# Residual rows kept in two load buffers, and the x and z normalizations on GpSimd

## The reference

```
x1  = x  + layernorm(recurrent(layernorm(x)))
out = x1 + layernorm(ffn(layernorm(x1)))

recurrent(v): u = v @ W_in.T + b_in                  # 512 -> 1024
              s[t] = tanh(u[t] + s[t-1] * gamma + beta)   # 1024 steps, elementwise
              y = s @ W_out.T + b_out                # 1024 -> 512
ffn(v):       z = ((silu(v @ gate_w * gate_scale)) * (v @ up_w * up_scale)) @ down_w * down_scale
                                                     # 512 -> 1536 -> 512
```

## Time and profile before

| | |
|---|---|
| Median of 3 runs | 625.39 us (625.18 to 625.69) |
| The profiled execution's own time | 625.78 us |
| Its span, first to last instruction | 624.0 us |
| Busy: PE, PEld | 528.8 us (85%), 449.0 us (72%) |
| Busy: DVE | 481.0 us (77%) |
| Busy: ACT | 310.6 us (50%) |
| Busy: POOL | 240.4 us (39%) |
| Mean granted TensorE clock | 0.937 |

### The profile page before, as it was taken

How to read it: one execution, slowest core, us unless ns; L and a number is a source line. 1 busy time by engine, 2 the same in 40 slices (tenths; PEclk the granted TensorE clock), 3 DMA queues, 4 the chain that set the end, 5 groups by cost and what they waited for, 6 DMA issues and landing times.

```text
span 624.0 us, 9844 instructions
## 1 busy us (share of the span) xinstructions
PE 528.8 (85%) x2880; PEld 449.0 (72%) x2880; DVE 481.0 (77%) x1832; ACT 310.6 (50%) x1442; POOL 240.4 (39%) x320
## 2 busy tenths in 40 slices
PE   4655232878999999999999999999999992999993
PEld 4644211568977998789878987799779971798992
DVE  4999997999778667966787679767886678675734
ACT  1354423365554755576546654665466544452330
POOL 2776672555224222422333332422342224243532
PEclk9957757789999999999999999999999996999997
DMA  7453440301010200110012001100001000100000
GB/s 235 128 171 123 124 141 29 90 29 52 1 35 1 69 1 1 35 67 2 1 34 69 1 2 34 56 14 0 2 3 65 2 0 2 67 2 2 1 35 34
DMA packets 16598, 27.47 MB, mean 44 GB/s; under 512 B 2336, under 2 KB 4512, under 8 KB 16544
## 3 DMA queue, kind: packets, MB, share of 16 engines
q1 hardware_dynamic: 16544, 26.84, 13.7%
HBM read 22.63 MB, written 4.19 MB: 43 GB/s over the span
## 4 chain that ended last, share of the span: by engine, by line
DVE 57%; ACT 21%; PE 14%; issue 3%; DMA 1%; SPq 1%; POOL 1%; POOLq 0%; DVEq 0%; ACTq 0%
DVE recur L634 23%; ACT pairs L922 10%; PE gate_up L528 7%; ACT pairs L909 4%; DVE fused L728 4%; ACT sigm L942 4%; DVE gated L721 3%; PE wide L553 3%; DVE peaks L780 3%; ACT fused_hi L957 3%; PE wide L493 2%; DVE rounder_own L776 2%; DVE y L675 2%; DVE z L793 2%; DVE x_in L658 2%
## 5 line engine op out<-in xcount | busy, mean ns | idle before, releaser
L922 ACT ACTIVATE pairs<-recur 128x16 f32<-128x16 f32 x1024 | 191.2, 187 | 249.5 <-DVE recur L634 247.1
L634 DVE TENSOR_TENSOR_SCAN recur<-recur,pairs 128x32 f32<-128x32 f32 x1024 | 234.4, 229 | 101.5 <-ACT pairs L922 100.1
L1025 POOL TENSOR_TENSOR fused_lo<-fused,fused_hi 128x256 fp32r<-128x256 f32 x96 | 71.1, 741 | 180.5 <-ACT fused_hi L957 180.4
L468 PE MATMUL wide<-x_norm_t,w_in_sb 128*128 128x256 f32 x448 | 106.6, 396 | 17.5 <-ACT pairs L909 13.2
L482 PE MATMUL wide<-w_out_sb,pairs 128*128 128x512 f32 x224 | 101.3, 606 | 22.1 <-DMA w_out_sb<-w_out_t 22.1
L468 PEld LDWEIGHTS wide<-x_norm_t,w_in_sb 128*128 128x128 f32 x448 | 87.6, 199 | 34.6 <-ACT pairs L909 15.4
L482 PEld LDWEIGHTS wide<-w_out_sb,pairs 128*128 128x128 f32 x224 | 65.5, 297 | 51.8 <-DMA w_out_sb<-w_out_t 22.5
L528 PE MATMUL gate_up<-x_hi,gate_q 128*128 128x256 f32 x384 | 96.8, 285 | 1.0 <-DVE fused L728 0.6
L528 PE MATMUL gate_up<-x_lo,up_q 128*128 128x256 f32 x384 | 96.0, 283 | 0.0
L528 PE MATMUL gate_up<-x_hi,up_q 128*128 128x256 f32 x384 | 95.6, 282 | 0.0
L528 PE MATMUL gate_up<-x_lo,gate_q 128*128 128x256 f32 x384 | 94.9, 281 | 0.0
(11 more groups left out here) (75 smaller groups left out, 640.2 us busy)
## 6 DMA issues: line engine op xcount, KB each, us to landing
x_in<-x SPq DMA_DIRECT2D x16, 256.0 KB, 3.1
x_res<-x SPq DMA_DIRECT2D x16, 256.0 KB, 3.1
out<-z SPq DMA_DIRECT2D x14, 256.0 KB, 2.4
raw_own<-gate_w SPq DMA_DIRECT2D x10, 256.0 KB, 2.8
raw_own<-down_w SPq DMA_DIRECT2D x9, 256.0 KB, 2.7
w_in_sb<-w_in_t SPq DMA_DIRECT2D x4, 512.0 KB, 6.8
raw_own<-up_w SPq DMA_DIRECT2D x8, 256.0 KB, 2.7
w_out_sb<-w_out_t SPq DMA_DIRECT2D x8, 256.0 KB, 2.9
```

The source lines that it names most:

```text
L468: ins = eng.matmul(wide[bank][:, jj * TOK:(jj + 1) * TOK], w_in_sb[:, k, j * P:(j + 1) * P], x_norm_t[:, k, :], start=(k == 0), stop=(k == ...
L634: eng.tensor_tensor_scan(preact[:, part(h), :].rearrange("p c k -> p (c k)"), factors[:, part(h), :].rearrange("p c k -> p (c k)"), pairs[ ...
L922: eng.activation(pairs[:, (n * T + t) % RING, part(h), 0], preact[:, part(h), 1], ACT.Tanh).then_inc(s_state[h], 1)
L1025: eng.tensor_tensor(fused_lo[:, f, :], fused[:, f, :], fused_hi[:, f, :].bitcast(F32), ALU.subtract).then_inc(s_fused_lo, 1)
```

## The change

There are two changes.

*Buffers.* x_res becomes two buffers, used by turns, and x1 stays in the one that its rows were loaded into until the tail has added it to z. The buffer x1 and the copy `keep_x1` go. The load into x_res of block n now waits for the tail of block n - 2.

*Engines.* The normalization of x of blocks 1 to 7 and that of z of blocks 0 to 6 go from VectorE to GpSimd, at the places that they had. On GpSimd each is one small instruction that negates the mean (128x1), and one that adds it and multiplies by the root, on the whole tile (128x512), where VectorE had two halves (128x256). The first block's x and the last block's z stay as they were. Semaphore counts follow (`x_normed`, `z_normed`).

```diff
-        x_res = sb("x_res", [P, batch, dim])
+        x_res = [sb(f"x_res{i}", [P, batch, dim]) for i in range(2)]
         y = sb("y", [P, batch, dim])
-        x1 = sb("x1", [P, batch, dim])
...
+        def x_normed(tile):
+            return 2 * (tile + 1) if tile < batch else batch + tile + 1
+
+        def z_normed(tile):
+            return tile + 1 if tile < batch * LAST else 2 * (tile + 1) - batch * LAST
...
             def load_residual(n, place):
                 yield place
-                if n > 0:
-                    eng.wait_ge(s_x1_kept, n)
-                    eng.wait_ge(s_x1_norm, 2 * batch * n)
+                if n >= 2:
+                    eng.wait_ge(s_out_ready, batch * (n - 1))
                 for b in range(batch):
-                    eng.dma_start(x_res[b:P:batch, :, :], x_blocks[n][b]).then_inc(s_x_res_in, 16)
+                    eng.dma_start(x_res[n % 2][b:P:batch, :, :], x_blocks[n][b]).then_inc(s_x_res_in, 16)
...
                     strands += [scale_z(n, b, at["z_copy"][b]),
                                 measure("z", z, n, b, at["z_halves"][b], at["z_whole"][b],
-                                        (s_z_scaled, 2 * (n * batch + b + 1))),
-                                normalize_z(n, b, at["z_norm"][b])]
+                                        (s_z_scaled, 2 * (n * batch + b + 1)))]
+                    if n == LAST:
+                        strands.append(normalize_z(n, b, at["z_norm"][b]))
...
                     strands += [measure_x(n + 1, b, BEFORE) for b in range(batch)]
-                    strands += [normalize_x(n + 1, b, BEFORE["x_norm"][b]) for b in range(batch)]
...
+            def normalize(w, rows, n, b, place, done):
+                yield place
+                tile = n * batch + b
+                eng.wait_ge(s_mv[w], tile + 1)
+                eng.tensor_scalar(minus_mean[w][:, b:b + 1], mean_var[w][:, b, 0:1], -1.0, 0.0, ALU.mult,
+                                  ALU.add).then_inc(s_minus_mean[w], 1)
+                eng.wait_ge(s_minus_mean[w], tile + 1 if w == "z" else tile - batch + 1)
+                eng.wait_ge(s_rstd[w], tile + 1)
+                eng.tensor_scalar(rows[:, b, :], rows[:, b, :], minus_mean[w][:, b:b + 1], rstd[w][:, b:b + 1],
+                                  ALU.add, ALU.mult).then_inc(done, 1)
+
...
-            def keep_x1(n, place):
-                yield place
-                eng.wait_ge(s_x1, batch * (n + 1))
-                if n > 0:
-                    eng.wait_ge(s_out_ready, batch * n)
-                eng.tensor_scalar(x1[:, :, :].rearrange("p b d -> p (b d)"),
-                                  x_res[:, :, :].rearrange("p b d -> p (b d)"), 0.0, 1.0, ALU.add,
-                                  ALU.mult).then_inc(s_x1_kept, 1)
...
                     strands.append(root("z", n, b, at["z_whole"][b]))
+                    if n < LAST:
+                        strands.append(normalize("z", z, n, b, at["z_norm"][b], s_z_norm))
                     if n < LAST or b < batch - 1:
                         strands.append(add_x1(n, b, at["z_norm"][b] + 1))
...
                     strands += [root("x", n + 1, b, BEFORE["x_whole"][b]) for b in range(batch)]
+                    strands += [normalize("x", x_in, n + 1, b, BEFORE["x_norm"][b], s_x_norm) for b in range(batch)]
...
-                    strands.append(keep_x1(n - 1, at["keep"]))
```

More of the change, by code:

```diff
@@ L48 @@
 AFTER = {"y": (0, 28), "y_copy": (23, 44), "y_norm": (30, 51), "r": (36, 56), "r_norm": (41, 61),
-         "t2": (57, 65), "t2_high": (57, 66), "keep": 68}
+         "t2": (57, 65), "t2_high": (57, 66)}
 FFN = 73
@@ L57 @@
 LAST_AFTER = {"y": (0, 28), "y_copy": (23, 44), "y_norm": (30, 51), "r": (36, 56), "r_norm": (41, 61),
-              "t2": (57, 64), "t2_high": (57, 65), "keep": 68}
+              "t2": (57, 64), "t2_high": (57, 65)}
 LAST_FFN = 85
 GROUP_AFTER = {"y": (66, 0), "x_res": 72, "y_copy": (87, 15), "y_norm": (97, 19.9), "r": (104, 23),
-               "r_norm": (110, 27), "t2": (32, 32), "t2_high": (32, 34), "keep": 60}
+               "r_norm": (110, 27), "t2": (32, 32), "t2_high": (32, 34)}
 END_USE = ((0, 0.3, 0.4, 1), (2, 2.3, 2.4, 3))
@@ L189, in recurrent_sandwich_kernel @@
         var_eps = {w: sb(f"var_eps_{w}", [P, batch]) for w in "xyrz"}
+        minus_mean = {w: sb(f"minus_mean_{w}", [P, batch]) for w in "xz"}
         rstd = {w: sb(f"rstd_{w}", [P, batch]) for w in "xyrz"}
@@ L227, in recurrent_sandwich_kernel @@
         s_var_eps = {w: sem(f"s_var_eps_{w}") for w in "xyrz"}
+        s_minus_mean = {w: sem(f"s_minus_mean_{w}") for w in "xz"}
         s_rstd = {w: sem(f"s_rstd_{w}") for w in "xyrz"}
@@ L426, in transpose_x @@
                     eng.wait_ge(s_ident_in, 16)
-                eng.wait_ge(s_x_norm, 2 * (tile + 1))
+                eng.wait_ge(s_x_norm, x_normed(tile))
                 if n >= 3:
@@ L685, in normalize_x1 @@
                             eng.wait_ge(s_t2, tile - batch + 1)
-                    eng.tensor_scalar(x1_norm[:, b, halves(half)], x_res[:, b, halves(half)],
+                    eng.tensor_scalar(x1_norm[:, b, halves(half)], x_res[n % 2][:, b, halves(half)],
                                       mean_var["r"][:, b, 0:1], rstd["r"][:, b:b + 1],
@@ L709, in residual_norm @@
                         normalize_y(n, b, at["y_norm"][b]),
-                        measure("r", x_res, n, b, (at["r"][b], at["r"][b] + 1), at["r"][b] + 2, (s_x1, tile + 1)),
+                        measure("r", x_res[n % 2], n, b, (at["r"][b], at["r"][b] + 1), at["r"][b] + 2, (s_x1, tile + 1)),
                         normalize_x1(n, b, at["r_norm"][b])]
@@ L764, in add_last_residual @@
                     if half == 0:
-                        eng.wait_ge(s_z_norm, 2 * batch * NB)
-                    eng.tensor_tensor(z[:, batch - 1, halves(half)], z[:, batch - 1, halves(half)], x1[:, batch - 1, halves(half)],
-                                      ALU.add).then_inc(s_last_ready, 1)
+                        eng.wait_ge(s_z_norm, z_normed(batch * NB - 1))
+                    eng.tensor_tensor(z[:, batch - 1, halves(half)], z[:, batch - 1, halves(half)],
+                                      x_res[LAST % 2][:, batch - 1, halves(half)], ALU.add).then_inc(s_last_ready, 1)
             def convert(first, end):
@@ L1008, in add_residual @@
                     eng.wait_ge(s_x_res_in, 16 * batch * (n + 1))
-                eng.tensor_tensor(x_res[:, b, :], y[:, b, :], x_res[:, b, :], ALU.add).then_inc(s_x1, 1)
-            def keep_x1(n, place):
-                yield place
-                eng.wait_ge(s_x1, batch * (n + 1))
-                if n > 0:
-                    eng.wait_ge(s_out_ready, batch * n)
-                eng.tensor_scalar(x1[:, :, :].rearrange("p b d -> p (b d)"),
-                                  x_res[:, :, :].rearrange("p b d -> p (b d)"), 0.0, 1.0, ALU.add,
-                                  ALU.mult).then_inc(s_x1_kept, 1)
+                eng.tensor_tensor(x_res[n % 2][:, b, :], y[:, b, :], x_res[n % 2][:, b, :], ALU.add).then_inc(s_x1, 1)
             def low_parts(n, use):
@@ L1034, in add_x1 @@
                 tile = n * batch + b
-                eng.wait_ge(s_z_norm, 2 * (tile + 1))
-                eng.tensor_tensor(z[:, b, :], z[:, b, :], x1[:, b, :], ALU.add).then_inc(s_out_ready, 1)
+                eng.wait_ge(s_z_norm, z_normed(tile))
+                eng.tensor_tensor(z[:, b, :], z[:, b, :], x_res[n % 2][:, b, :], ALU.add).then_inc(s_out_ready, 1)
             def tail(n, at):
@@ L1083, in _ @@
             weave(low_parts(LAST - 1, {**end_use, **use_places(END_FFN, LAST_CHUNKS, KI, beside=False)}),
-                  *tail(LAST - 1, END_TAIL), *residual_norm(LAST, 1, GROUP_AFTER), keep_x1(LAST, GROUP_AFTER["keep"]),
+                  *tail(LAST - 1, END_TAIL), *residual_norm(LAST, 1, GROUP_AFTER),
                   low_parts(LAST, use_places(GROUP_FFN, 0, KI, beside=False)))
```

1 line of the change is left out of this document (removed).

## The result

| | before | after |
|---|---|---|
| median of the runs taken side by side | 625.43 us (625.07 to 626.18, 20 runs) | 626.46 us (625.17 to 627.26, 20 runs) |
| span of the profiled execution | 624.0 us | 624.9 us |
| VectorE instructions, busy | 1832, 481 us | 1776, 461 us |

The ratio is 1.0016 with a 95% interval of 1.0009 to 1.0022: the changed kernel is 0.16% slower, 1.0 us. The forecast was 0.5 us faster. The time lies in the forecast's wide range (621.9 to 627.6), outside its narrower one (624.0 to 626.1), and the sign is the other way, though still within the 0.2% that the forecast called no change. All ratios here are of runs in the fast state, so that two runs of the kernel before, of 1888 us, taken beside e1 to e4, are left out.

What follows compares the result with a forecast made beforehand. The recurrence, scan and tanh in turn, was taken to set the pace, with TensorE the other limit; 0.6 (blocks 2 to 7) less 0.2 (block 0) plus 0.1 (block 1), 0.5 off 625.39, gave 624.9 us, range 621.9 to 627.6.

Steps and rivals of the forecast that it cites:

- The long step at place 53: Blocks 2 to 7: z's first half (L749), shut out by GpSimd's add, makes a step 0.92 too long; it goes.
- The root's wait: Second tile's x1 normalization (L686) waits for its root behind z's normalization on GpSimd; takes back 0.56 of the 0.92.
- The second half shut out: L686's second half starts inside GpSimd's normalization of z's second tile, ends at 268.46; 0.10 a block is left.
- first rival: L686's second half is not shut out: 0.36 saved a block, 623.1 us; chance 0.20.
- The price of the normalization: GpSimd's 128x512 normalization taken as 0.62 us from L1016, between bounds of 0.62 and 1.27.
- rival of a dearer normalization: GpSimd's normalization costs more than 0.62, counting twice a block: 628.9 us at 0.95, 632.7 at 1.27; chance 0.15.
- Its port rule: Skill's rule: only VectorE's 2-port modes and ops with two SBUF inputs want the port lock; other L686 would run free.
- x in the steady blocks: Blocks 2 to 5: x's two normalizations take 2 us on GpSimd, some 10 us ahead of the transposes; worth nothing.
- the buffers: Two x_res buffers let residual loads start earlier, but the add reading them comes 30 places later; worth nothing.
- the end: GpSimd's low parts: the fifth shifts to about 594.4, TensorE needs it at 598.67; worth nothing.
- Block 0 and block 1: Block 0 loses about 0.2 to the shut-out weight conversion; block 1 removes 1.2 of long L658 but keeps 0.1.
- TensorE as a limit of 0.91 a block: TensorE idles 0.91 in block 3, so a block can't win more than about 0.9 whatever VectorE does.

Runs made afterwards that it cites:

- e1: Kernel before with two x_res buffers and without the copy keep_x1, all normalizations still on VectorE: 625.20 us, ratio 0.9997.
- e4: Changed kernel with GpSimd's root of x1 for the second tile ahead of z's first-tile normalization, no wait added: 627.34 us, ratio 1.0033.
- e2: Changed kernel with GpSimd's normalization using immediates 0.0 and 1.0 instead of columns, leaving those rows unnormalized: 624.38 us, ratio 0.9979.
- e6: Changed kernel with z's normalization back on VectorE in all blocks, only x on GpSimd: 625.75 us, ratio 1.0006.
- e10: Changed kernel with 32 one-column memsets on VectorE, where it idles before the first load: 626.38 us, ratio 1.0016.
- e8: e1 with VectorE normalizing z at places 63 to 66 and GpSimd adding both tiles after that: 619.84 us, ratio 0.9904.
- e5: e4 with GpSimd normalizing and adding both z tiles only after the second tile's x1 normalization, blocks 2 to 7: 620.81 us, ratio 0.9926.
- e7: e5 with x's normalization back on VectorE in all blocks: 619.76 us, ratio 0.9909.

## Why the forecast was wrong, by its own steps

*The long step at place 53.* Right: gone in all six blocks, 0.92 in block 3.

*The root's wait.* Right in kind. The forecast had L686 start at 267.33; it started at 267.45, because the normalization took 0.77 and not 0.62, less 0.03 of gaps that were shorter.

*The second half shut out.* Right against its first rival: it wanted to start at 267.91, 0.12 into L1018, and lasted 0.79. Forecast end 268.46, measured 268.70, before 268.56. The dearer normalization counts a second time here: 0.15 twice, less 0.06 of smaller terms, is the 0.24 between the two ends. The forecast missed one thing in its favour: the scan behind a shut-out instruction starts 0.07 before that one's recorded end, as it did behind L749.

*The price of the normalization: the step that failed.* "I take 0.62, since L1016 is the same operation; only the scalars come from columns." The columns were the difference: 0.768 for z, 0.617 with immediates in e2. L1016 has immediates. The price is what moved the second half's end by 0.24 in block 3; six times that is 1.4 us on a saving of 0.6, and with the 0.07 above a block comes out about even, as the 0.96 against 0.92 shows. This is the forecast's own rival of a dearer normalization, to which it gave 0.15. e2 confirms it from the other side, and shows that the smaller terms erred the other way: with the price as forecast, the two steps of block 3 are 0.91 and 0.68, 0.63 too long, which saves 0.29 of the 0.92, where the forecast had 0.10. The Trainium skill, GPSIMD Engine Reference, section 3.1, gives 768 ns by its rate and 769 ns as measured for 512 elements in the best case of its loop (the forecast put these together as 768 measured). With columns the trace agrees, with a mean of 768 in the group of z; with immediates the same instruction took 617 (e2), less than that best case. The forecast's estimate by that page, 626.7, is 0.2 from the measured 626.46, and that is partly luck, since the smaller terms and the odd steps, which it did not have, about cancel.

*Its port rule.* The other page, SBUF — State Buffer, section Who interferes with whom, lets instructions outside VectorE's 2-port modes and with one SBUF input run free of the lock. L693 reads one tensor from SBUF, and its mean and root from two 128x1 columns, and takes 0.39 for 256 elements. That is the time of the statistics on as many (L651, 0.40). VectorE's max and multiply with immediates (L792) takes about as long for 512:

```profile
63.76 0.42 DVE L792 TENSOR_SCALAR rounder_own<-rounder_own 128x512 f32<-128x512 f32 x1
```

So L693 shows no doubled rate, and it was shut out all the same (0.79, 0.83 and 1.30), while L651 was not (0.40 at 264.81). No view shows the mode it runs in, and no run tells whether the columns count as inputs, so whether the rule fails here stays open. The forecast went by the row of L749 and was right to.

*x in the steady blocks, the buffers, the end.* Nothing that can be told, as forecast: e1 and e6 are level with before. The time from the start of the last scan to the end of the span is 64.1 us in one profile and 64.2 in the other.

*Block 0 and block 1.* The lock on L799 (L807 after) was forecast at 0.2 and was 0.42 (0.83 for 0.41):

```profile
36.25 0.81 POOL L1018 TENSOR_SCALAR x_in<-x_in,minus_mean_x,rstd_x 128x512 f32<-128x512 f32 x1
...
36.50 0.83 DVE L807 TENSOR_TENSOR gate_q<-z 128x256 fp32r<-128x256 f32 x1
```

In block 1 the 1.2 us of long L658 are gone and GpSimd's queue gave the time back, as worked out: L682 waits 0.94 for its root.

```profile
116.90 0.55 POOL L1007 TENSOR_TENSOR rstd_y<-var_eps_y,minus_half 128x1 f32<-128x1 f32 x1
...
117.48 0.41 DVE L682 TENSOR_SCALAR y<-y,mean_var_y,rstd_y 128x256 f32<-128x256 f32 x1 [0.94 <-POOL rstd_y L1007]
```

Forecast 0.1 saved, measured 0.1 lost. These two blocks differ between kernels that do the same there (block 1 took 70.50 after, 69.70 in e10), so tenths in them are not to be explained.

*What the sum did not have.* The odd steps, 0.64 us in the profile after. The whole distance is 1.4 us: 0.5 off the span was forecast, and 0.9 more was measured. It is made up of 0.8 in blocks 2 to 7 (0.2 lost where 0.6 was to be saved), 0.64 in the odd steps, 0.2 in each of blocks 0 and 1, less the 0.40 by which the first scan came earlier. That last one is no effect of the change that can be named: over the kernels here the first scan starts anywhere from 24.7 to 25.8.

*TensorE as a limit of 0.91 a block.* Neither refuted nor tested: the best version, e8, gives 5.57 in six blocks, 0.93 a block. TensorE is busy 64.8 of the 65 us from 237 to 302 us in e5, e7 and e8, against 64.1 before, so little more is to be had there.

## What to carry to other kernels

Moving streaming work off a busy engine onto GpSimd gains nothing where the engine's gaps were free already; look for the few instructions that stick out of the gaps, and ask first whether their place can change (e8: 1% for three lines on top of e1, with no work moved to another engine). In a queue that is served in order, what stands ahead of a small op costs its length as soon as another engine waits for that op (e2: 0.15 off the normalization took 0.16 off the wait). A new op beside a shared lock has to be placed so that the other engine's instructions don't start inside it: e4 took away the wait only, and lost; e5 took away wait and overlap, and won 0.7%. And a price read from an op "of the same kind" must match in its operands: immediates or columns.

## What was unexpected of the hardware

- GpSimd's add and multiply on 128x512 takes 0.617 us with immediates (e2) and 0.768 with both scalars from 128x1 columns.
- VectorE's 128x256 normalization, 0.39 free, is shut out by a one-input GpSimd op as well as by a two-input one: 0.79 under L1018, 0.83 when it starts 0.09 behind L1018's start, 1.30 behind L1045. Each time it ends 0.14 to 0.15 after the GpSimd op. The statistics of 256 elements (L651, 0.40) and the scans (0.23) run at their usual length under the same op.
- Single steps of the chain take 0.28 to 0.35 longer at places that move with the number of instructions ahead of them on VectorE (step 125, 120 or nowhere in block 3). The late record is number 704, 832, 960, 1344, 1472 or 1600 of VectorE's in the trace. Where it is a gate product, the trace has no releaser for it but "issue". A transfer of the instruction queue starts 0.2 us behind the step in block 3 of the kernel after (at 301.3). That the fetch of code is the cause was not tested.
